# Last graph layer: TensorE takes over two sums of rotation products and one sum over v, in PSUM with the identity

## The reference

```python
R = relu(edge_weight[:, None] @ w1 + b1) @ w2 + b2        # E x 384 radial weights
# per edge: features of the source, 8 scalars and 8 vectors of 3
msg = sum over v, f of NORM * R[u, v, f] * Y[f] * F[v, i] * C[o, f, i]
out[dst] += msg
x = layernorm(x + out)
```

## Time and profile before

| what | value |
|---|---|
| median of 3 runs | 18773.71 us (18770.79 to 18778.72) |
| the profiled execution: its time | 18780.07 us |
| its span, first to last instruction | 18778.3 us |
| DVE busy, share of the span | 13743.4 us, 73% |
| POOL busy, share of the span | 12860.4 us, 68% |
| PE matmul busy, share of the span | 5929.7 us, 32% |
| ACT busy, share of the span | 3023.8 us, 16% |
| mean granted TensorE clock | 0.694 |
| the last layer's groups, first to last mA | 13766.3 to 18556.6 us |

### The profile page before, as it was taken

The page is one execution under the profiler, slowest core; times in us unless marked ns, Lnnn a source line. Parts: engine busy times, 40 slices in busy tenths (PEclk is TensorE's granted clock), DMA queues, the critical chain, the costliest instruction groups (busy, mean ns, idle before and its releaser), DMA issues. The chain is left out here.

```text
span 18778.3 us, 129812 instructions
## 1 busy us (share of the span) xinstructions
PE 5929.7 (32%) x26457; PEld 3816.1 (20%) x26457; DVE 13743.4 (73%) x18503; ACT 3023.8 (16%) x4191; POOL 12860.4 (68%) x13055
## 2 busy tenths in 40 slices
PE   0111111110444444443400000000046666666663
PEld 0000000000333333332300000000024444444442
DVE  4777777772999999997933333333379999999995
ACT  0000000000222222220011111111112222222221
POOL 3777777776677777774057777777766666666665
PEclk9999965555777777776555555555567777777776
DMA  4333333331111111112322222222212222222221
GB/s 111 97 97 97 97 97 97 97 97 28 30 28 28 28 28 28 27 28 73 144 61 59 59 59 59 59 59 59 46 42 47 46 46 45 46 47 46 45 45 28
DMA packets 815992, 1106.80 MB, mean 59 GB/s; under 512 B 441715, under 2 KB 577705, under 8 KB 802674
## 3 DMA queue, kind: packets, MB, share of 16 engines
q0 software_dynamic: 437600, 503.25, 12.3%
q1 hardware_dynamic: 302643, 403.03, 7.8%
q10 hardware_dynamic: 75474, 197.60, 2.8%
HBM read 714.37 MB, written 389.45 MB: 59 GB/s over the span
## 5 line engine op out<-in xcount | busy, mean ns | idle before, releaser
L1642 POOL DMA_INDIRECT s_arena<-d_t,s_arena x6250 | 5903.2, 945 | 2087.2 <-issue 2020.9
L1620 POOL DMA_INDIRECT s_arena<-d_t,s_arena x3125 | 3250.5, 1040 | 1547.9 <-issue 915.1
L1518 PE MATMUL psall<-s_w2r,s_arena 128*128 128x384 f32 x6250 | 3175.2, 667 | 1873.9 <-DVE s_arena L949 1636.5
L1597 POOL DMA_INDIRECT d_pay<-s_arena x3125 | 3027.0, 969 | 992.4 <-issue 930.7
L1518 PEld LDWEIGHTS psall<-s_w2r,s_arena 128*128 128x128 f32 x6250 | 1946.9, 324 | 3101.8 <-DVE s_arena L949 2225.9
L1428 PE MATMUL psall<-s_arena 128*128 128x500 bf16 x1875 | 872.8, 493 | 4191.3 <-DVE s_arena L530 3793.3
L958 DVE TENSOR_REDUCE s_arena<-s_arena 128x96 f32<-128x1536 f32 x1125 | 1819.2, 1627 | 0.0
L896 DVE TENSOR_TENSOR s_arena<-s_arena,psall 128x2400 f32<-128x2400 f32 x125 | 332.0, 2656 | 1735.2 <-DMA s_arena<-d_t,s_arena 1735.2
L1363 ACT ACTIVATE s_arena<-s_arena 128x800 f32<-128x800 f32 x250 | 428.6, 1714 | 6220.2 <-DVE s_arena L1096 6220.2
L1542 PE MATMUL psall<-s_tails,s_mfix 128*128 128x32 f32 x6 | 1.9, 412 | 3987.3 <-DVE s_tails L1104 3987.3
L1428 PEld LDWEIGHTS psall<-s_arena 128*128 128x128 bf16 x1875 | 198.9, 106 | 4761.6 <-DVE s_arena L530 4206.6
(11 more groups left out here) (270 smaller groups left out, 12432.9 us busy)
## 6 DMA issues: line engine op xcount, KB each, us to landing
s_arena<-d_t,s_arena POOLq DMA_INDIRECT x9375, 2.5
d_scan<-s_arena ACTq DMA_DIRECT2D x375, 400.0 KB, 2.5
s_arena<-d_ew SPq DMA_DIRECT2D x126, 800.0 KB, 6.5
s_arena<-d_pay SPq DMA_DIRECT2D x33, 1650.0 KB, 7.2
d_inj<-s_agg SPq DMA_DIRECT2D x125, 400.0 KB, 4.0
s_arena<-d_inj SPq DMA_DIRECT2D x125, 400.0 KB, 3.5
d_pay<-s_arena POOLq DMA_INDIRECT x3125
d_pay<-s_agg SPq DMA_DIRECT2D x100, 429.0 KB, 3.0
```

The lines of the kernel that those rows point to most:

```text
L1518: e.matmul(ps[BANK[g] + t][:, 0:384], hv_[:, :, t0 + t], w2r[:, :], start=True, stop=True).then_inc(sem("pe_r"), 1)
L1597: e.indirect_dma_start(pay_d, bass.IndirectOffsetOnAxis(ap=S1.adr[s4][:, t:t + 1], axis=0), S1.pay[s4][:, 33 * t:33 * t + 33], None).then_ ...
L1620: e.indirect_dma_start(L3.gb[s][:, t], None, T3_d, bass.IndirectOffsetOnAxis(ap=L3.idx[s][:, t:t + 1], axis=0)).then_inc(sem(f"g3_{s}"), 16)
L1642: e.indirect_dma_start(L.gb[s][:, t * L.CW:(t + 1) * L.CW], None, L.tab, bass.IndirectOffsetOnAxis(ap=L.idx[s][:, t:t + 1], axis=0)).then_ ...
```

## The change

Three things change in the last layer, and with them the order of the work.

1. **Rotation sums.** PE adds the three products of each rotation, with the identity as the stationary operand and the products (600 floats on each partition) as the moving one, in two matmuls of 512 and 88 columns for each product, which accumulate in PSUM (L3.rot, bank 5 and part of 6). ba, bs, aa and ag are gone from DVE. ACT now reads the sums from PSUM: scalar_vectors3 is new and writes the turned-back vectors into the scan's input, and scalar_split3 reads L3.rot.
2. **Sums over v.** For groups 0 and 2 the products lie in L3.prodP, and PE sums over v: over_v has 16 matmuls of 6 x 32 = 192 columns, one for each v, with the identity as the stationary operand; the moving operand is every 16th float of prodP. r0 and r2 are gone from DVE. ACT copies the sums into L3.sums (scalar_sums3, new).
3. **Groups.** Ten groups of three and two tiles in turn replace eight of three and one of one.

PE's order in a chunk is R0 R1 R2 B0 R3 R4 B1 R5 B2 R6, half of over_v, R7, the other half, R8 A0 A1 R9 A2, where R is a radial group, B a back product and A an along product.

```diff
+        L3.prodP = agg[:, 0:3072].rearrange("p (t c) -> p t c", t=6)
-        GROUPS = [(3 * g, 3) for g in range(8)] + [(24, 1)]
-        BANK = [3 * (g % 2) for g in range(8)] + [6]
+        GROUPS = [(5 * (g // 2) + 3 * (g % 2), 3 - g % 2) for g in range(10)]
+        BANK = [3 * (g % 2) for g in range(10)]
+        ONPE = (0, 2)
+        L3.rot = psall[:, 2560:2560 + T * 24]
+        L3.vs = ps[6][:, 96:288]
...
-        ORDER = ("mA0 mB0 mA1 mB1 r0 bk0 mA2 mB2 r1 bk1 mA3 mB3 r2 bk2 ba mA4 mB4 r3 ca bs mA5 mB5 r4 sc al0 al1 "
-                 "mA6 mB6 r5 al2 aa mA7 mB7 r6 ag mA8 mB8 r7 r8").split()
+        ORDER = ("mA0 mB0 mA1 mB1 bk0 mA2 mB2 r1 bk1 mA3 mB3 bk2 mA4 mB4 r3 mA5 mB5 r4 al0 mA6 mB6 r5 ca sc al1 "
+                 "mA7 mB7 r6 al2 mA8 mB8 r7 mA9 mB9 r8 r9").split()
...
+        def scalar_vectors3(e, c, k):
+            e.wait_ge(sem("pe_b"), c + 2)
+            e.activation(L3.sit[(k - 1) % 2][:, :, 8:32], L3.rot.rearrange("p (t f) -> p t f", t=T), ACT.Copy).then_inc(sem("ac_B"), 1)
+        def scalar_sums3(e, c, k):
+            e.wait_ge(sem("pe_v"), c + 2)
+            e.activation(L3.sums[k % 2][:, 0:10].rearrange("p (a b) c -> p a (b c)", a=2)[:, :, 0:96],
+                         L3.vs.rearrange("p (a w) -> p a w", a=2), ACT.Copy).then_inc(sem("ac_V"), 1)
...
+        def tensor_turn3(e, buf, j, name):
+            for a, b in ((0, 512), (512, T * 24)):
+                m = e.matmul(L3.rot[:, a:b], ident[:, :], buf[j][:, a:b], start=j == 0, stop=j == 2, skip_group_check=True)
+            if j == 2:
+                m.then_inc(sem(name), 1)
...
+            def radial(g):
+                t0, n = GROUPS[g]
+                if g == 0:
+                    e.wait_ge(sem("ac_h"), c + 1)
+                e.wait_ge(dv.h, v3(c, f"mB{g - 2}") if g > 1 else v3(c - 1, f"mB{g + 8}"))
...
+            def over_v(part):
+                if part == 0:
+                    e.wait_ge(dv.h, v3(c, "mB2"))
+                    e.wait_ge(sem("ac_V"), c + 1)
+                    e.wait_ge(sem("ac_B"), c + 2)
+                for v in range(4 * part, 4 * part + 4):
+                    m = e.matmul(L3.vs.rearrange("p (t b) -> p t b", t=6), ident[:, :], L3.prodP.rearrange("p t (b v) -> p t b v", v=16)[:, :, :, v],
+                                 start=v == 0, stop=v == 15, skip_group_check=True)
```

More of the change, by code:

```diff
@@ L353, in gnn_kernel @@
         L3.row = [cv(32 * T) for _ in range(2)]
-        L3.prod = [cv(3 * 512).rearrange("p (t c) -> p t c", t=3) for _ in range(3)]
+        L3.prod = [cv(3 * 512).rearrange("p (t c) -> p t c", t=3) for _ in range(2)]
+        L3.prodP = agg[:, 0:3072].rearrange("p (t c) -> p t c", t=6)
         L3.sums = [cv(T * 32).rearrange("p (t c) -> p t c", t=T) for _ in range(2)]
@@ L955, in red @@
                 done(f"mB{g}")
-                if g == 0:
-                    e.wait_ge(sem("ac_0"), c)
+                if g == ONDVE[0]:
+                    e.wait_ge(sem("ac_B"), c + 1)
                 e.tensor_reduce(L3.sums[s2][:, t0:t0 + n].rearrange("p t c -> p (t c)"),
-                                L3.prod[g % 3][:, 0:n].rearrange("p t (b v) -> p (t b) v", v=16), AX.X, ALU.add).then_inc(dv.up(), 1)
+                                prod(g).rearrange("p t (b v) -> p (t b) v", v=16), AX.X, ALU.add).then_inc(dv.up(), 1)
             def along(j):
+                if last:
+                    skip(f"al{j}")
+                    return
                 if j == 0:
@@ L964, in along, with back @@
                     e.wait_ge(sem("ac_M"), c + 2)
-                    done_before("ag")
+                    e.wait_ge(sem("pe_a"), c + 1)
                 along3(e, k + 1, j).then_inc(dv.up(), 1)
[L968 to L971, removed]
+            def back(name):
+                if first:
+                    skip(name)
+                else:
+                    vector_back3(e, c, k, name)
             mul(0)
             mul(1)
-            red(0)
-            back_("bk0")
+            back("bk0")
             mul(2)
             red(1)
-            back_("bk1")
+            back("bk1")
             mul(3)
-            red(2)
-            back_("bk2", "ba")
+            back("bk2")
             mul(4)
             red(3)
-            back_("ca", "bs")
             mul(5)
             red(4)
[L987 to L992, removed]
+            along(0)
             mul(6)
             red(5)
[L995 to L1000, removed]
+            back("ca")
+            back("sc")
+            along(1)
             mul(7)
             red(6)
[L1003 to L1009, removed]
+            along(2)
             mul(8)
             red(7)
+            mul(9)
             red(8)
+            red(9)
         def vector_back3(e, c, k, name):
@@ L1049, in vector_edges3 @@
                 along3(e, 0, j).then_inc(dv.up(), 1)
[L1050 to L1054, removed]
             mk["base3"] = dv.n
@@ L1318, in scalar_chunk3 @@
                 scalar_hidden3(e, i, k + 1, c + 1)
+            if not first:
+                scalar_vectors3(e, c, k)
+            if not last:
                 e.wait_ge(dv.h, v3(c, "bk2"))
@@ new lines, in tensor_chunk3, with back, along @@
+        def tensor_chunk3(e, c, k, first=False, last=False):
+            hv_ = L3.HS[k % 2].rearrange("h (p t) -> h p t", p=P)
+            def radial(g):
[3 more added lines that the diff above has]
+                e.wait_ge(dv.h, v3(c, f"mB{g - 2}") if g > 1 else v3(c - 1, f"mB{g + 8}"))
+                for t in range(n):
+                    m = e.matmul(ps[BANK[g] + t][:, 0:384], hv_[:, :, t0 + t], w2r[:, :], start=True, stop=True)
+                m.then_inc(sem("pe_r"), 1)
+            def back(q):
+                if first:
+                    return
+                if q == 0:
+                    e.wait_ge(sem("ac_G"), c + 1)
+                e.wait_ge(dv.h, v3(c, f"bk{q}"))
+                tensor_turn3(e, L3.bp, q, "pe_b")
+            def along(j):
+                if last:
+                    return
+                if j == 0:
+                    e.wait_ge(sem("ac_B"), c + 2)
+                    e.wait_ge(sem("ac_V"), c + 2)
+                e.wait_ge(dv.h, v3(c, f"al{j}"))
+                tensor_turn3(e, L3.gp, j, "pe_a")
+            def over_v(part):
+                if part == 0:
+                    e.wait_ge(dv.h, v3(c, "mB2"))
+                    e.wait_ge(sem("ac_V"), c + 1)
+                    e.wait_ge(sem("ac_B"), c + 2)
+                for v in range(4 * part, 4 * part + 4):
+                    m = e.matmul(L3.vs.rearrange("p (t b) -> p t b", t=6), ident[:, :], L3.prodP.rearrange("p t (b v) -> p t b v", v=16)[:, :, :, v],
+                                 start=v == 0, stop=v == 15, skip_group_check=True)
+                if part == 3:
+                    m.then_inc(sem("pe_v"), 1)
+            radial(0)
+            radial(1)
+            radial(2)
+            back(0)
+            radial(3)
+            radial(4)
+            back(1)
+            radial(5)
+            back(2)
+            radial(6)
+            over_v(0)
+            over_v(1)
+            radial(7)
+            over_v(2)
+            over_v(3)
+            radial(8)
+            along(0)
+            along(1)
+            radial(9)
+            along(2)
@@ L1520, in tensor_edges3 @@
         def tensor_edges3(e):
-            e.sem_inc(sem("pe_r"), 50)
+            e.sem_inc(sem("pe_r"), 20)
+            e.sem_inc(sem("pe_b"), 2)
+            e.sem_inc(sem("pe_v"), 1)
             barrier(e, "tensor")
-            tensor_chunk3(e, 0, 0)
-            with e.Fori(0, 31) as i:
+            for j in range(3):
+                e.wait_ge(dv.h, mk["base3"] - 2 + j)
+                tensor_turn3(e, L3.gp, j, "pe_a")
+            tensor_chunk3(e, 0, 0, first=True)
+            with e.Fori(0, 30) as i:
@@ L1525, in tensor_edges3 @@
                 for k in range(1, 5):
                     tensor_chunk3(e, i * 4 + k, k)
+            for k in range(1, 5):
+                tensor_chunk3(e, 120 + k, k, last=k == 4)
+            for q in range(3):
+                e.wait_ge(dv.h, v3(125, f"bk{q}"))
+                tensor_turn3(e, L3.bp, q, "pe_b")
         def tensor_edges(e, layer):
```

69 lines of the change are left out of this document (34 added, 35 removed).

## The result

The changed kernel takes 18443.13 us (median of 4 runs, 18436.28 to 18449.97) against 18772.34 for the kernel before: a ratio of 0.9824, 95% interval [0.9807, 0.9841], or 329 us less. The forecast was 18520 us, 256 less, in a range of 18180 to 18800. The profiled execution has a span of 18443.5 us.

A forecast was written before the change was run, and what follows sets the result against it. DVE's instruction sum bounded the last layer; PE's circle would bound it after. Chunk 38.35 to 36.3 us, times 125, saves 256 us: 18780 less 256 is 18524, stated as 18520, range 18180 to 18800.

The forecast's parts named there:

- DVE's saving: DVE's work in the last layer falls from 38.35 to 32.0 us a chunk, with 4.3 us of waits, mostly at mA8.
- PE becomes the bound, by a circle: PE's order R2 to R9 takes 30.0 us, the way back through DVE to R2 6.2: 36.2 a chunk.
- The step: over_v reading every 16th float costs 1.84 ns a column, 0.354 us a pass, 11.3 us for 32 passes.
- The other terms of the circle: On PE from R2 to R9: 20 tiles in 40 radial passes 13.2 us, five turns 5.5 us.
- The 0.1 for the clock: Added to the 36.2 us chunk for a clock that falls now and then, giving 36.3.
- The two ends of the difference: Chunk length before, 38.35 us, and after, 36.3 us; times 125 chunks, 256 us saved.
- The clock: PE, busy 34.4 of 36.3 us, was expected fast nearly always, with granted clock above 0.95.
- The rival in which strided passes let it fall: over_v may not count as activity, so some ten later passes run slow: chunk 39.4 us, 18905 us; chance 0.12.
- the reading that 1.75 and even 2.44 us of idle time leave it fast: PE idle that long before a group stayed at the fast level; after 3.96 us it was slow.
- The rival of a free step: over_v costs 5.3 us by columns alone; chunk 32.6 to 34.4 us, 18055 to 18280 us; chance 0.20.
- "Only bk0 of the next chunk needs" the sums over v: ACT's copy of the sums follows over_v and was taken as hidden, needed only by bk0 on DVE.
- the forecast's upper bound of 32.6: POOL needs 31.2 us a chunk for gathers, up to 32.6 when the scan holds one 1.4 us longer.

The follow-up runs named there:

- A1 behind R9: Changed kernel with the turn of al1 moved on PE from in front of R9 to behind it; ratio 0.9781 to the kernel before, 34.88 us a chunk.
- The experiment that takes the step away: Changed kernel with over_v reading 32 floats in a row instead of every 16th float; ratio 0.9696 to the kernel before, 33.58 us a chunk.
- the lighter ones: Follow-up kernels where PE's work took less time than in the changed kernel, such as summing only group 0 over v on PE (0.9814).
- the fastest version: Changed kernel plus v outermost in products, six idle matmuls before R2, sums copied before the scan's row, r1 ahead of mA2; ratio 0.9607, 18059.35 us.
- group 0 alone: Changed kernel with only group 0 summed over v on PE and group 2 back on DVE; ratio 0.9814 to the kernel before, 35.31 us a chunk.

## Why the prediction was right

- **DVE's saving.** 32.0 us of work a chunk were forecast, and waits of 4.3. Measured are 909.6 of 1,000 us busy, which is 32.3 of a chunk of 35.51, and 3.2 of waits, most of them at mA8 as forecast: 1.97 there, 0.66 at mA9 and 0.55 at mA2.
- **PE becomes the bound, by a circle.** Right, and shown by A1 behind R9. Forecast 30.0 + 6.2; read 29.4 + 6.2 (R2 at 16017.90, A2 at 16047.33, R2 at 16053.56).
- **The step.** The mechanism was right and the size 9% too high: 0.354 forecast from two weight loads, 0.324 measured, 1.69 ns a column; without the step it is 0.84. Over 32 passes that is 0.9 us a chunk.
- **The other terms of the circle.** The five turns took 5.3 instead of 5.5. The radial groups went the other way, 13.8 instead of 13.2: a pass of 384 columns is 0.322, but a group whose first weight load follows a turn takes 0.16 more (16021.11 to 16024.49 is ten passes and 0.16), four times on the circle, and R2 behind its idle time 0.23 more. The sum didn't have that. So part of the nearness of 30.0 to 29.4 is errors that cancel. The 0.1 for the clock wasn't needed.
- **The two ends of the difference.** The forecast took 38.35 for the chunk before, edges included; between scans it is 38.20. The saving was 2.69 a chunk instead of 2.05, hence 329 us instead of 256.
- **The Trainium skill's rules.** That each access to another line pays (Advanced Engine Details and Errata, "SBUF Cachelines") is borne out by 0.324 against 0.162 us. Counting a pass by its columns alone (TensorE: Matmul & The Clock Gate, "Back-to-back issue gap") holds here for contiguous reads only, and at another price: its formula gives 0.42 ns a column, these float32 passes take 0.84.
- **The clock.** Full speed all through, as forecast: R2 was fast in 122 of 123 chunks behind 1.55 us of idle time. The rival in which strided passes let it fall is refuted, since over_v ran for 10.4 us of each chunk at 1.00. But the reading that 1.75 and even 2.44 us of idle time leave it fast was taken from rows that fitted. The same view of the kernel before has the same two pauses with the other outcome:

```profile
16004.29 4.02 PE L1518 MATMUL psall<-s_w2r,s_arena 128*128 128x384 f32 x6 [1.75 <-DVE s_arena L949]
...
16085.75 3.60 PE L1518 MATMUL psall<-s_w2r,s_arena 128*128 128x384 f32 x6 [2.44 <-DVE s_arena L949]
```

  Over that whole layer, six passes behind a pause of 1 to 2 us were wholly fast in 127 of 257 cases, behind 2 to 3 us in 28 of 230, behind more in none of 136. It didn't matter in the changed kernel; it mattered in all that made PE lighter.
- **The rival of a free step** would have given 32.6 to 34.4 a chunk. The experiment that takes the step away gave 33.6, so its price was right too, the clock's share included.
- **ScalarE.** "Only bk0 of the next chunk needs" the sums over v was wrong: along(0) on PE waits for ac_V too. In the changed kernel A0 never waits for it; in the lighter ones it did, for 1.3 to 1.7 us.
- **POOL.** It waited for DVE 4.3 us a chunk, where some 4 were forecast. Its gathers lasted 945 ns on average, and only six of 3,125 lasted over 1.2 us, so the scan held almost none: in this rhythm POOL mostly waits while the scan runs. In the fastest version, where POOL is the bound as well, 121 gathers last over 2 us, about one a chunk, and the chunk of 32.3 lies below the forecast's upper bound of 32.6.

## What to carry to other kernels

Before work goes to an idle engine, follow its order of work in a circle through the waits, not only its sum: here 34 us of PE work made a chunk of 35.6, and a move of one turn within the same work gave 0.4%. A sum over a middle index with the identity should read its moving operand in a row; if need be permute the weights that produce it, which costs nothing at run time but one more DVE instruction for each group here. Where TensorE waits at a fixed point of a loop and its next group is on the critical path, matmuls without use in the pause can pay for themselves. And where a reading of the clock rests on a few rows, count all of the layer's: here rows with the same pause showed both levels.

## What the hardware showed

A float32 pass that reads every 16th float costs exactly twice a contiguous one, 0.324 against 0.162 us for 192 columns, while weight loads with a step of 25 floats had let 1.84 ns a column be expected. Six idle matmuls a chunk took the granted clock from 0.96 to 1.00 and 0.7% off the whole kernel. The same pause left the next group at either level: behind idle time of 2.2 us R2 was wholly fast in 40 of 123 chunks with contiguous reads and in 41 of 123 with group 0 alone. What decides between them stays open.

In the last layer of the kernel before, a gather that overlaps one of the adds with both inputs in SBUF (ba, bs, aa, ag) is held: the median of 437 is 1.28 us instead of 0.94. One that overlaps the scan takes 2.31 (129 of them). Of the 2,559 others a single one took over 1.1.
